# Graph attention over sorted edges: plain stores in place of scattered empty rows, and loads of the first sum split over two queues

## What is computed

```python
K, Q, V = (typed_linear(x, W, b, node_type) for (W, b) in ((Wk, bk), (Wq, bq), (Wv, bv)))
e0, e1, e2 = (cos(log(t + 1)[:, None] * w_time + b_time) for t in (ea[:, 0], ea[:, 1], ea[:, 2]))
att,   v   = edge_msgs(K[row], Q[col], V[row], e1, e2)
att_i, v_i = edge_msgs(K[col], Q[row], V[col], e2, e1)
att   = seg_softmax(att, col, n)
att_i = seg_softmax(att_i, row, n)
agg = segment_sum([v * att, e0], col) + segment_sum([v_i * att_i, e0], row)
y = typed_linear([agg, agg], Wa, ba, node_type) + x
out = layernorm(x + layernorm(y) * gamma[type] + beta[type])
```

## Time and profile before

| | us |
|---|---|
| three runs | 9465.21, 9444.9, 9433.6 |
| their median | 9444.9 |
| the profiled execution's own time | 9428.41 |
| its span, first to last instruction | 9426.7 |
| busy: PE, PEld | 6161.3, 4258.6 |
| busy: DVE, ACT, POOL | 6590.5, 4318.3, 5663.1 |
| mean granted TensorE clock | 0.726 of full |

### The profile page before, as it was taken

How to read it: one execution, slowest core, us unless ns; L and a number is a source line. 1 busy time by engine, 2 the same in 40 slices (tenths; PEclk the granted TensorE clock), 3 DMA queues, 4 the chain that set the end, 5 groups by cost and what they waited for, 6 DMA issues and landing times. The chain is left out here.

```text
span 9426.7 us, 136983 instructions
## 1 busy us (share of the span) xinstructions
PE 6161.3 (65%) x33872; PEld 4258.6 (45%) x33873; DVE 6590.5 (70%) x13978; ACT 4318.3 (46%) x13153; POOL 5663.1 (60%) x5439
## 2 busy tenths in 40 slices
PE   4786666666663777777776777740566637399947
PEld 2674444444442444444444444420455526277734
DVE  2799999999994666666666666643455537688855
ACT  0003434444342555555555555531455527399933
POOL 6406777777775777777777777756788850000014
PEclk7655555555555888888888888875789879699975
DMA  4100000000003888888888888885999999488851
GB/s 161 68 0 9 9 9 9 9 9 9 9 9 111 265 260 261 262 261 262 261 260 259 259 260 261 260 227 173 312 336 330 336 195 202 139 260 262 260 188 55
DMA packets 1360145, 1670.61 MB, mean 177 GB/s; under 512 B 418411, under 2 KB 1159769, under 8 KB 1359593
## 3 DMA queue, kind: packets, MB, share of 16 engines
q1 hardware_dynamic: 854746, 958.02, 31.2%
q0 software_dynamic: 260288, 671.32, 23.1%
q10 hardware_dynamic: 244944, 39.68, 3.6%
HBM read 1064.62 MB, written 641.81 MB: 181 GB/s over the span
## 5 line engine op out<-in xcount | busy, mean ns | idle before, releaser
L1124 PE MATMUL exch_pG<-exch_tab,exch_ohT 128*128 x3328 | 1535.0, 618 | 937.8 <-ACT exch_kc L1046 934.3
L1547 PE MATMUL sum_pS<-sum_row,sum_oh 128*128 128x260 f32 x6656 | 1658.0, 405 | 696.9 <-issue 278.4
L991 POOL DMA_INDIRECT exch_row<-table,exch_of x1664 | 1676.7, 1008 | 546.5 <-issue 506.8
L836 POOL DMA_INDIRECT recs<-place_rec,place_addr x1568 | 1576.6, 1005 | 505.3 <-issue 481.6
L1547 PEld LDWEIGHTS sum_pS<-sum_row,sum_oh 128*128 128x128 f32 x6656 | 1296.1, 200 | 1058.5 <-issue 859.4
L1124 PEld LDWEIGHTS exch_pG<-exch_tab,exch_ohT 128*128 128x128 f32 x3328 | 769.1, 243 | 1683.9 <-issue 1490.9
L1586 DVE TENSOR_TENSOR sum_row<-sum_row,agg_al 128x1792 f32<-128x1792 f32 x416 | 841.6, 2023 | 496.4 <-DMA sum_row<-spill 489.1
L1205 POOL DMA_INDIRECT bys<-sum_pb x768 | 942.9, 1228 | 272.2 <-issue 225.4
L1205 POOL DMA_INDIRECT bys<-exch_pb x832 | 838.5, 1008 | 311.8 <-issue 249.8
L1569 ACT ACTIVATE sum_off<-kept_ramp,sum_neg 128x128 f32<-128x128 f32 x3328 | 1017.6, 388 | 0.0
L718 PE MATMUL place_pB<-place_rows,sort_sel 64*128 64x512 bf16 x784 | 464.7, 593 | 660.9 <-DVE place_junk L790 660.7
(11 more groups left out here) (293 smaller groups left out, 11861.8 us busy)
## 6 DMA issues: line engine op xcount, KB each, us to landing
spill<-exch_row SPq DMA_DIRECT2D x208, 1024.0 KB, 5.1
sum_row<-spill SPq DMA_DIRECT2D x208, 1024.0 KB, 8.1
sum_row<-bys SPq DMA_DIRECT2D x208, 1024.0 KB, 5.0
mid<-exch_pb SPq DMA_DIRECT2D x208, 528.0 KB, 4.5
sum_pb<-mid SPq DMA_DIRECT2D x192, 528.0 KB, 4.8
exch_row<-table,exch_of POOLq DMA_INDIRECT x1664
recs<-place_rec,place_addr POOLq DMA_INDIRECT x1568
bys<-exch_pb POOLq DMA_INDIRECT x832, 3.4
```

The costliest lines, as they stand in the source:

```text
L836: nc.gpsimd.indirect_dma_start(recs, bass.IndirectOffsetOnAxis(addr[:, par, 0, t:t + 1], 0), rec[:, par, t, :], None, bounds_check=last_sl ...
L991: nc.gpsimd.indirect_dma_start(row[q][:, t, TD:TD + S.TW], None, table, bass.IndirectOffsetOnAxis(of[q][:, t:t + 1], 0), bounds_check=last ...
L1124: nc.tensor.matmul(pG[t % 3][:, 0:VK], ohT[ring(j, 2)][:, t, :], flat[:, bass.ds(tiles[t] * GW, VK)], start=True, stop=True).then_inc(s_ga ...
L1547: last = nc.tensor.matmul(pS[h * HG + t // 2][:, 0:AW], oh[h][:, t, :], row[j][:, t, :], start=(t % 2 == 0), stop=(t % 2 == 1))
```

## The change

1. `count_owners` no longer computes the slots of empty rows. It keeps one small vector, `tails`: for each owner the number of its last tile but one.
2. `place_edges`: ACT's copy and POOL's indirect DMA of empty rows are gone. SyncE, which had nothing to do there, stores `none` to the array's last FREE = 102 columns of tiles in one DMA, and then, one after another, each waiting for the landing of the one before, to the two columns that begin at each owner's `tails`. Edges overwrite what belongs to them later, in `exchange` and after.
3. First sum: there are no `ONLY` and `BOTH` stretches. SyncE loads the rows of steps 0 and 1 and then only forwarded blocks, all 192; then it waits for all to have landed and issues the eight loads of `runs_crd`. ACT issues the row load of step n + 2 in its own step n, between the wait on `s_p` and the one-hot's last operation. The second sum's loads stay on SyncE.

```diff
@@ count_owners (DVE)
-            dve.wait_ge(s_prep, 2)
-            link(nc.vector.tensor_copy(pad[:], pad_i[:]))
-            link(nc.vector.tensor_scalar(pad_off[:], pad[:], float(S.NPAD), float(1 << 20), ALU.is_ge, ALU.mult))
...
                 if d:
-                    link(nc.vector.tensor_tensor_scan(st[:, 2, :], st[:, 4, :], zero[:, 0:NO], 0.0, ALU.add, ALU.add))
...
-                    link(nc.vector.tensor_tensor(pad_ge[:], bc(pad[:], 2, NO), bc(st[:, 1, :], 1, NPC), ALU.is_ge))
-                    link(nc.vector.tensor_tensor(pad_ge[:], pad_ge[:], bc(st[:, 4, :], 1, NPC), ALU.mult))
-                    link(nc.vector.tensor_reduce(pad_s[:], pad_ge[:], op=ALU.add, axis=AX))
...
+                    link(nc.vector.tensor_scalar(tails[:], st[0:1, 2, :], -2.0, 0.0, ALU.add, ALU.max))
@@ place_edges
+        @block.sync
+        def _(sp):
+            rows_of = bys.rearrange("(p c) f -> p c f", p=P)
+            sp.wait_ge(s_none, 2)
+            sp.dma_start(rows_of[:, NT - S.FREE:NT, :], bc(none[:], 1, S.FREE)).then_inc(s_clear, 16)
+            for o in range(0, NO, 7):
+                n = min(7, NO - o)
+                _, at = nc.values_load_multi_w_load_instructions(
+                    tails[0:1, o:o + n], engines=[nc.sync.engine], min_val=0, max_val=NT - 2,
+                    skip_runtime_bounds_check_because="an owner's last tiles")
+                for i, c in enumerate(at):
+                    sp.wait_ge(s_clear, 16 * (o + i + 1))
+                    sp.dma_start(rows_of[:, bass.ds(c, 2), :], bc(none[:], 1, 2)).then_inc(s_clear, 16)
+            sp.wait_ge(s_clear, 16 * (NO + 1))
...
-                act.wait_ge(s_scat[par], i * (16 * (SG + 1)))
-                nc.scalar.activation(pad_at[:, par, :], k.padslot[:, bass.ds(g, 1)], ACT.Copy)
+                act.wait_ge(s_scat[par], i * (16 * SG))
...
-                pad(pad_at[:, par, :], s_scat[par])
@@ aggregate
+    def load(eng, n, j):
+        eng.dma_start(row[j][:, :, 0:VW], rows_v[:, bass.ds(n * G, G), 0:VW]).then_inc(s_v[j], 16)
...
+        for n in range(2 if bys is not None else 4):
+            load(nc.sync, n, n)
         if bys is not None:
-            with sp.Fori(0, ONLY // 4) as i:
+            with sp.Fori(0, (NS - SKIP) // 4) as i:
                 for j in range(4):
-                    passed(4 * i + j + SKIP, j, i)
...
+                    sp.wait_ge(s_sc[j], 16 * S.LATER * i)
+                    sp.dma_start(pb[j][:], mid[:, bass.ds((4 * i + j + SKIP) * G + S.NOW, S.LATER), :]).then_inc(s_pb[j], 16)
+            v = bys.rearrange("(p c) f -> p c f", p=P)
+            for j in range(4):
+                sp.wait_ge(s_sc[j], 16 * S.LATER * ((NS - SKIP) // 4))
+            for a in range(0, NT, NT // 8):
+                sp.dma_start(crd[:, a:a + NT // 8, :], v[:, a:a + NT // 8, S.SC:S.SC + H + 1]).then_inc(s_x, 16)
+            sp.wait_ge(s_x, 16 * 8)
@@ aggregate (ACT, in a step)
             act.wait_ge(s_p, n * HG)
+            if bys is not None and left >= 2:
+                load(nc.scalar, n + 2, (j + 2) % 4)
             nc.scalar.activation(oh[h][:], off[:], ACT.Relu, bias=1.0, scale=-1.0).then_inc(s_oh, 1)
-        rounds(act, step, scores_back)
+        rounds(act, step)
```

More of the change, by code:

```diff
@@ L433, in sort_edges @@
         s = Scope(nc, ctx, "sort")
-        k.padslot = s.sb("padslot", [P, S.NPC], I32)
+        tails = s.sb("tails", [1, S.NO], I32)
         own = s.sb("own", [P, 2, CT])
@@ L445, in sort_edges, with count_owners @@
         base = s.sb("base", [P, 2, S.LN, NO])
[L446 to L451, removed]
+        count_owners(nc, k, S, src, dst, edge_attr, recs, otile1, tails, own, piece, inval, ln, ramp_hi, oh_lo, oh_hi, tri, sel, block4, base)
+        place_edges(nc, k, S, recs, bys, tails, own, piece, inval, ln, ramp_hi, oh_lo, oh_hi, tri, sel, block4, base)
+def count_owners(nc, k, S, src, dst, edge_attr, recs, otile1, tails, own, piece, inval, ln, ramp_hi, oh_lo, oh_hi, tri, sel, block4, base):
+    CT, CE, REST, SG, NO, NT = S.CT, S.CE, S.REST, S.SG, S.NO, S.NT
     NG = CT // SG
@@ L470, in count_owners @@
         junk = s.sb("junk", [P, NO])
[L471 to L477, removed]
         pH = [s.pb(f"pH{d}") for d in range(2)]
@@ L618, in _, with place_edges @@
                 last.then_inc(s_ot, 1)
-def place_edges(nc, k, S, recs, bys, own, piece, inval, ln, ramp_hi, oh_lo, oh_hi, tri, sel, block4, base):
+def place_edges(nc, k, S, recs, bys, tails, own, piece, inval, ln, ramp_hi, oh_lo, oh_hi, tri, sel, block4, base):
     CT, SG, NO, NT, REC, LN = S.CT, S.SG, S.NO, S.NT, S.REC, S.LN
@@ L1485, in aggregate, with rounds @@
         s_turn = s2.sem("turn")
-    def rounds(eng, step, middle=None):
-        if BOTH:
-            with eng.Fori(0, BOTH // 4) as i:
-                for j in range(4):
-                    step(4 * i + j, j, i, 5)
-        if middle is not None:
-            middle()
-        with eng.Fori(BOTH // 4, NS // 4 - 1) as i:
+    def rounds(eng, step):
+        with eng.Fori(0, NS // 4 - 1) as i:
             for j in range(4):
@@ L1513, in _, with step @@
     def _(sp):
[L1514 to L1516 removed]
+        for n in range(2 if bys is not None else 4):
+            load(nc.sync, n, n)
         if bys is not None:
[L1519 removed]
+            with sp.Fori(0, (NS - SKIP) // 4) as i:
                 for j in range(4):
[L1521 to L1535 removed]
+                    sp.wait_ge(s_sc[j], 16 * S.LATER * i)
[6 more added lines that the diff above has]
+            sp.wait_ge(s_x, 16 * 8)
+        else:
+            def step(n, j, i, left):
+                if left >= 4:
+                    sp.wait_ge(s_p, (n + 2) * HG)
+                    load(nc.sync, n + 4, j)
+            rounds(sp, step)
     @block.tensor
@@ L1554, in _ @@
     def _(act):
-        def scores_back():
-            if bys is not None:
-                v = bys.rearrange("(p c) f -> p c f", p=P)
-                for j in range(4):
-                    act.wait_ge(s_sc[j], 16 * S.LATER * ((NS - SKIP) // 4))
-                for a in range(0, NT, NT // 8):
-                    nc.scalar.dma_start(crd[:, a:a + NT // 8, :], v[:, a:a + NT // 8, S.SC:S.SC + H + 1]).then_inc(s_x, 16)
         def step(n, j, i, left):
```

48 lines of the change are left out of this document (4 added, 44 removed).

## The result

| | before | after |
|---|---|---|
| median of the runs shown, us | 9447.9 (4 runs) | 9294.2 (4 runs) |
| profiled execution: span, us | 9426.7 | 9278.5 |
| first empty-row memset of `place_edges` | 713.5 | 698.8 |
| first record load of `exchange` | 2957.2 | 2891.2 |
| first load of the first sum | 6508.7 | 6448.0 |

The ratio is 0.9839, 95% interval 0.9827 to 0.9852: 152 us of 9448 saved by the ratio, 154 by the medians, where 217 were forecast. 9294 lies in the range, 66 us above the predicted 9228. By differences of the table's rows, the start gained 14.7 us, `place_edges` 51.3, the first sum 98.7 (1515.4 to 1416.7 us). `exchange` and the first softmax took 5.3 us longer, the second sum 7.7 (836.9 to 844.6 between its first and last load), the output 2.9.

A forecast was written before the change was run, and what follows sets the result against it. POOL, never resting, was taken to bound `place_edges`, and SyncE's waits for forwarding the first sum. Gains of 12 + 106 + 99 = 217 us from 9428.4 gave 9211, plus 16.5 a median of 9228 us; range 9130 to 9345.

The forecast's parts named there:

- The start: In `count_owners`, eleven DVE operations go, and DVE then waits for PE's matmuls: gain 12 us.
- `place_edges`: POOL loses one DMA of 17 per group, 22.28 us becoming 21.2: gain 106 us, range 67 to 125.
- held by DVE and the landing: Rival in `place_edges`: group time 21.9 us instead of 21.2, gain 37 us, median 9297; chance 0.08.
- POOL waiting for DVE in most groups: Sign in `place_edges` that would show the forecast wrong; no size given.
- The clearing: SyncE's added stores in `place_edges`, some 200 us for all, run where SyncE and DMA are idle: cost 0.
- First sum: Forwarding takes 1219 us, ending at 7737; next stage's first copy at 7925 instead of 8024.08: gain 99 us, bounds 28 and 136.
- the DMA is the wall: Rival in the first sum: DMA, not SyncE's order, limits; stage gains 28 to 74 us, median say 9270; chance 0.13.
- Crowding: Rival in the first sum: row loads are served ahead of forwarding, 318 us lost, 9645 in all; chance 0.05.
- the first two signs of being wrong: First sum: a step time of 5 us with POOL waiting for `sum_pb`; steps left over at the end of `runs_crd`.
- ACT never idle for 100 us: Sign in the first sum that would show the forecast right: no ACT idle stretch of 100 us.

The follow-up runs named there:

- the later wait: Changed kernel with ScalarE's wait for the landing in `place_edges`, and the four record copies, moved behind the group's second counters: 9263.6 us, ratio 0.9789.
- the short lead: Kernel before with only `LEAD`, the forwarded blocks SyncE loads ahead of the first row, cut from 32 to 4: 9382.9 us, ratio 0.9918.
- the weights in PSUM: Changed kernel with the first sum's weights copied by ScalarE to a PSUM bank, from where VectorE's multiplication reads them: 9102.5 us, ratio 0.962.
- The sort alone: Changed kernel with the old `aggregate` and `LEAD` back at 32, so only the empty rows are handled anew: 9402.4 us, ratio 0.9934.
- the clearing twice: Changed kernel with each of SyncE's 50 clearing stores issued twice, one after the other: 9317.3 us, ratio 0.9849.
- the one with both edits: Changed kernel with ScalarE's `place_edges` wait behind the second counter copies and the first sum's weights read from PSUM: 9082.6 us, ratio 0.9602.
- the sum alone: Kernel before with only the new `aggregate`, the first sum's new loads: 9388.2 us, ratio 0.9911.
- the empty row first: Kernel before with each group's empty-row DMA issued ahead of the 16 record DMAs instead of behind them: 9517.7 us, ratio 1.006.

## Why the prediction was right, and where its terms were off

*The start*, 12 us: 14.7 measured, the eleven operations as named (DVE waits 5.77 us for PE, then copies at 694.87).

*`place_edges`*, 106 us: 51. This is the term that failed, and its lower bound of 67 too. The working had the loop's price, "two groups in 42.7 us, 21.4 each", next to POOL's alone, 21.0, and took 21.2, between them; the measured period is 21.71. Both prices were low. The loop is no bound to be averaged with another: it came to 43.0 and it held, since in 83 of 98 groups POOL started 0.80 to 0.90 us after its address was written, and in none sooner. POOL alone is not 21.0 either: by the table above its DMAs are stretched by 0.89 us per group where 21.0 had carried over the 0.54 of before, and it pauses for 0.26 that was nowhere in the trace of before. The run with the later wait has the loop open and still takes 21.30, 92 us less than before for the stage, so even then not 106. What gained was 97 x 0.58 = 56 us, and 5 of them are lost again behind the last group, where the next stage's first load comes 12.5 us after POOL's last DMA instead of 6.9; why, stays open. The rival "held by DVE and the landing", 21.9 and 37 us, had the mechanism, and forecast and rival lie on either side of the 51. The test named for it, "POOL waiting for DVE in most groups", came out that way: an address was ready under 0.9 us before POOL's start in 83 of 98.

*The clearing*, 0: right to a few us; the trace has it over after 160 us, where 265 were reckoned (45 for the large store, 2.4 each for the small).

*First sum*, 99 us: 98.7, but out of terms that miss and cancel. The ceiling of 334 GB/s was none: 379 is what was moved once the rows were uncoupled, so steps took 4.5 us instead of 6.4 and all 208 weighings, not 190, fell on the forwarding. A weighing cost 280 / 208 = 1.35 us instead of 1.24 (before, counted in the same way, 196 / 162 = 1.21), and 8 us more went to four DMAs beside the sum's last multiplications, also with two operands in SBUF. Together with a start that was 11 us behind the first load instead of 10, forwarding ended 1280 us after it instead of 1228: 51 or 52 lost. Against that nothing was left to run beside `runs_crd`, and from there to the copy it took 137 us instead of the 188 reckoned (3 + 152 + 30 + 3): 51 won. That the stage came out at 98.7 is luck. What the forecast rested on, that forwarding under DVE's stalls is the path and the lead has to go, is what the short lead and the weights in PSUM show. The rival "the DMA is the wall" fell in the changed kernel, where the share is 0.65 for the last 300 us of forwarding and POOL's DMAs are the path; it came near only where the stall was gone.

*Crowding*, the slower rival: rows did run first, but forwarding did not starve. POOL waited 49.6 us for its blocks, 46.8 before, and by 7400 us, with the rows over, 518 of 768 DMAs had been issued, where 65 blocks, 260 DMAs, were the point of decision.

*The signs.* The matmuls did begin 16 us after the stage's first load, SyncE's eight loads came last, and neither of the first two signs of being wrong appeared. "POOL waiting for DVE in most groups" did. "ACT never idle for 100 us" failed: with the rows over at 7395, ACT stood idle for 476 us, until the next stage. These us are the room that the weights in PSUM then used.

## What to carry to other kernels

When two engines wait for each other through a landing, add up the whole loop and take it as it stands, even where the busiest engine in it shows waits of only 0.1 to 0.2 us. Look for a place behind work that needs nothing from the wait: moving it there gained 40 us of `place_edges`, where one DMA fewer in the loop had gained 51. Where a queue of small DMAs on GpSimd is the path, look for DMAs of uneven length beside VectorE operations with two SBUF operands: 32 values a partition, copied to PSUM in each step, took 288 us off the forwarding and 2.2% off the kernel. Before a redesign, try the constant: cutting `LEAD` from 32 to 4 gained most of what the new loads did. Then ask again how the work is split, since the old split was made with the stall in it.

## What the hardware showed that was not expected

Rows and forwarding issued from separate engines moved 379 to 386 GB/s for over 900 us, where the same bytes in one waiting order moved 334 with a DMA share of 0.98: that share was no sign of a full DMA.

In `place_edges` of the changed kernel, POOL pauses behind its 113th, 225th, 337th ... DMA, 13 times, always 112 apart and always with "issue" for a releaser. This is the 114th:

```profile
883.30 0.97 POOL L813 DMA_INDIRECT recs<-place_rec,place_addr  x1 [2.23 <-issue]
```

Seven groups are 112 DMAs. The groups with the pause take 22.7 us or a little more where the others take 21.56 on average, 16 us in the stage. The sort alone, the weights in PSUM and the clearing twice, with 16 DMAs a group too, pause at the same DMAs; so do the one with the later wait and the one with both edits, mostly for 1.1 to 1.7 us. The kernel before, the sum alone and the empty row first, with 17 a group, pause nowhere. What it is stays open.

An indirect DMA of 973 ns became 2.70 us long beside one VectorE instruction of 2.03 us; in both examples above it ends 0.83 to 0.84 us behind that instruction's end. So do 207 of the 208 DMAs that met a weighing in the changed kernel's first sum: 0.84 to 0.85 us behind its end, wherever in the DMA the weighing began.
